# Choice over clusters kept in the PSUM bank of its logits, and new orders of steps for all engines

## The chip, the cores and the metric

The program runs on one core of one Trainium2 chip. The metric is the device time of one execution in microseconds, as the median of several runs. The core has five engines with a queue of instructions each: TensorE (PE in the profile), VectorE (DVE), ScalarE (ACT), GpSimd (POOL) and SyncE (SP), which here only issues loads and stores. ScalarE's queue issues some transfers too.

## What is computed

A layer on x of four batches of 512 tokens with 512 features (f32), in four stages, each of them `x = x + f(layernorm(x))`:

```python
attn = jnp.einsum('ds,td->st', w1, w2) * sparse_mask          # stage 1
y = jnp.einsum('bds,st->bdt', x, attn) + b2; gelu(y)
# stages 2 and 4 (the same weights)
dots = softmax(x @ centroids.T / 0.1, axis=-1)                # 64 clusters
hits = dots > 0.01
query_sel = any(hits, axis=1); cluster_sel = any(hits, axis=0)
dense = x @ weight.T + bias
out = where(query_sel[:, None] & cluster_sel[assignments][None, :], dense, 0)
# stage 3: attention with one head of 128: qkv, softmax(q k^T) v, Wo
```

`cluster_sel` is over all 2048 tokens of a stage, so the mask of the output columns is known only when the last batch's probabilities are.

## The kernel before

A tile is 128 tokens of one batch by 512 features; there are 16, named `b.t` (batch, tile). f32 products are made from three matmuls of operands split into a high and a low part (`products`, L1011 to L1020): high by high, low by high, high by low. A **chunk** is one block of 128 of the contraction, so three matmuls of 128x512.

What each engine does, and in which order, is written out in tables of steps: PE_ORDER, ACT_ORDER, DVE_ORDER, POOL_ORDER, SP_ORDER (loads and the stores issued by SyncE), AQ_ORDER (loads that ScalarE's queue issues first) and AS_ORDER (stores that it issues last). Each engine goes through its table strictly in order; a step waits on semaphores for what it needs (`done_at`). The names of the steps that matter here:

- `load.w1.c`, `load.w2.c`, `load.x0.t`: the loads of 256 KB with which the kernel starts. `w1hi.c`, `w2hi.c` (ScalarE, L590 and L586) copy the high part, `w1lo.c`, `w2lo.c` (VectorE) make the low one.
- `attn.c`: 12 matmuls of the product of the two weights (attn.0 in three parts of four); `last.i` ends that product for rows i.
- `stats`, `rstd`, `norm.s.b.t` (VectorE, GpSimd, ScalarE L613): layernorm of a tile; `T.xs.b.t` (TensorE, L1113): its transposition, four blocks into one of four rotating banks `t_bank`; `hi.x`, `lo.x` (ScalarE L645, VectorE L824) split it. `T.x2`, `T.x4` transpose what the stages 1 and 3 left, and their norm is applied after the product.
- `y1.b.t.cNN`, `dn2`, `dn4`: chunks NN of the products of the stages 1, 2 and 4 in one of four rotating banks `m_bank`; `dn4h.3.3.h` are the two halves of the last tile. The bank is freed by `x1`, `ev2`, `blend4`.
- The choice, for stage s (2 or 4) and batch b: `cls.b` (TensorE, L1197) makes the logits, 64 high and 64 low rows by 512 tokens; `lgev` (ScalarE, L681) copies them; `tc.s.b` (TensorE, L1119) transposes them into a `t_bank`; `logit` (VectorE, L930) adds high and low into `cl`; `lmax` (L935, L937) takes the maximum; `cexp` (ScalarE, L703) writes the exponentials into `ce`; `prob` (L944 to L954) sums, divides and takes the running maximum over batches. `best1` (L959), `bestT` (TensorE), `csel` and `mask.2`, or `tmask.4` and `masks.4` (L1138), then make the mask of the output columns.
- The end: `qb` and `xb` (ScalarE L755, GpSimd L559) put bias and residual together, `blend4` (L977) adds the product. For 11 tiles and the halves VectorE then copies by the mask (`out`, L1001; `outh`, L994); for the four tiles of BY_POOL GpSimd does it in two steps, `pm` (L565) with the mask in `rows` (ScalarE, `rows4`, L713), and `pa` (L570).

TensorE starts with WARM matmuls on constants (L1009), before any load has landed.

The body of prob before:

```python
link(dve.tensor_reduce(out=csum[:, :], in_=ce[:, :, :], op=ALU.add, axis=AX.X))
link(dve.reciprocal(crec[:, :], csum[:, :]))
dve.tensor_scalar(chosen, crec[:, :], THRESHOLD, None, ALU.is_gt).then_inc(chosen_done, 1)
```

(`link` makes VectorE wait for the instruction's own end.)

## Time and profile before

| | us |
|---|---|
| median of 3 runs (275.39 to 275.49) | 275.45 |
| the profiled execution | 275.24 |
| its span, first to last instruction | 273.4 |
| TensorE busy (1397 matmuls) | 268.8 |
| VectorE busy | 192.2 |
| ScalarE busy | 177.0 |
| GpSimd busy | 163.8 |

All times inside the span count from its start. Matmuls overlap each other in the trace, so that what one costs is read from the distance of the starts, not from its duration. Idle time of an engine matters only where TensorE, or the last store, waits for it.

### The profile page before, as it was taken

What the parts mean: (1) busy time and instruction counts of PE and PEld (TensorE: products, weight loads), DVE (VectorE), ACT (ScalarE), POOL (GpSimd) and SP (SyncE); (2) the same over time, 40 slices, a digit from 0 to 9 for tenths busy, and PEclk for the clock granted to TensorE, in tenths of its full rate; (3) what the DMA queues carried; (4) which work ended last, traced back from release to release, by engine and by line L of the source; (5) the groups of instructions that cost most, each with busy time, mean ns of one, the idle gap of its engine ahead of it and who ended that gap; (6) DMA issues with size and microseconds to landing.
All of it is one profiled execution on the core that took longest, in us unless ns stands there. A gap on an engine that the chain in (4) does not pass through costs nothing.

```text
span 273.4 us, 4428 instructions
## 1 busy us (share of the span) xinstructions
PE 268.8 (98%) x1397; PEld 225.6 (82%) x1397; DVE 192.2 (70%) x406; ACT 177.0 (65%) x359; POOL 163.8 (60%) x196
## 2 busy tenths in 40 slices
PE   8999999999999999999999999999999999999995
PEld 8787888888888888788988888888888888887784
DVE  3988988605935867794478796788447584875994
ACT  3855886455477786448889988779544747577500
POOL 4883988265395491189896993990541247102795
PEclk9999999999999999999999999999999999999999
DMA  7999064800000000000000000000000000000096
GB/s 253 372 362 326 14 219 167 305 4 2 0 0 0 2 0 2 0 2 0 2 0 0 1 4 0 0 2 0 2 2 0 0 2 0 1 2 0 36 361 220
DMA packets 10247, 18.25 MB, mean 67 GB/s; under 512 B 1200, under 2 KB 1968, under 8 KB 10224
## 3 DMA queue, kind: packets, MB, share of 16 engines
q1 hardware_dynamic: 8784, 15.47, 16.2%
q10 hardware_dynamic: 1440, 2.49, 2.5%
q8 instruction: 12, 0.20, 0.3%
q14 instruction: 11, 0.09, 0.1%
HBM read 13.76 MB, written 4.19 MB: 66 GB/s over the span
## 4 chain that ended last, share of the span: by engine, by line
PE 96%; DMA 1%; DVE 1%; POOL 1%; issue 0%; ACT 0%; DVEq 0%; POOLq 0%
PE m_bank L1018 76%; PE t_bank L1113 12%; PE m_bank L1197 6%; PE t_bank L1119 1%; DMA x_tok<-in_L_attn_a_x 1%; PE m_bank L1073 1%; ACT xn_odd L613 0%; PE t_bank L1138 0%; DVE st L817 0%; POOL rstd L471 0%; POOL ve L470 0%; DVE y_tok L988 0%; DVE x_tok L994 0%; PE m_bank L1144 0%; PE t_bank L1124 0%
## 5 line engine op out<-in xcount | busy, mean ns | idle before, releaser
L1018 PE MATMUL m_bank<-ffn_hi,even_hi 128*128 128x512 f32 x96 | 38.9, 406 | 0.0
L1018 PE MATMUL m_bank<-ffn_lo,even_hi 128*128 128x512 f32 x96 | 37.6, 392 | 0.0
L1018 PE MATMUL m_bank<-ffn_hi,even_lo 128*128 128x512 f32 x96 | 37.4, 390 | 0.0
L602 ACT ACTIVATE ones_and_squares<-x_tok,mv 128x512 bf16<-128x512 f32 x44 | 31.6, 717 | 4.1 <-DVE x_tok L921 3.7
L559 POOL TENSOR_TENSOR y_tok<-y_tok,x_tok 128x512 f32<-128x512 f32 x12 | 15.3, 1289 | 25.6 <-ACT y_tok L755 25.6
L539 POOL TENSOR_TENSOR y_tok<-y_tok,bias_f 128x512 f32<-128x512 f32 x16 | 20.6, 1295 | 16.2 <-ACT y_tok L696 16.2
L467 POOL TENSOR_SCALAR ve<-mv 128x1 f32<-128x1 f32 (+1 forms) x20 | 5.3, 264 | 37.9 <-ACT ones_and_squares L602 36.9
L824 DVE TENSOR_TENSOR even_lo<-t_bank,even_hi 128x512 fp32r<-128x512 f32 x24 | 16.2, 684 | 12.8 <-ACT even_hi L645 12.6
L471 POOL TENSOR_TENSOR rstd<-ve,half 128x1 f32<-128x1 f32 (+1 forms) x31 | 23.5, 758 | 2.6
L824 DVE TENSOR_TENSOR odd_lo<-t_bank,odd_hi 128x512 fp32r<-128x512 f32 x28 | 18.8, 686 | 6.4 <-ACT odd_hi L645 6.2
L1018 PE MATMUL m_bank<-odd_hi,wqkv_hi 128*128 128x512 f32 (+1 forms) x60 | 21.5, 358 | 0.0
L1018 PEld LDWEIGHTS m_bank<-ffn_lo,even_hi 128*128 128x128 f32 x96 | 18.0, 188 | 3.9
L1018 PE MATMUL m_bank<-odd_lo,wqkv_hi 128*128 128x512 f32 (+1 forms) x60 | 20.9, 349 | 0.0
L553 POOL TENSOR_TENSOR x_tok<-x_tok,bo 128x512 f32<-128x512 f32 x16 | 20.9, 1322 | 0.0
L1018 PE MATMUL m_bank<-odd_hi,wqkv_lo 128*128 128x512 f32 (+1 forms) x60 | 20.8, 347 | 0.0
L1018 PEld LDWEIGHTS m_bank<-ffn_hi,even_lo 128*128 128x128 f32 x96 | 18.1, 189 | 3.1
L1018 PEld LDWEIGHTS m_bank<-ffn_hi,even_hi 128*128 128x128 f32 x96 | 18.1, 188 | 3.0
L613 ACT ACTIVATE xn_odd<-x_tok,ve,rstd 128x512 f32<-128x512 f32 x20 | 16.1, 811 | 5.8 <-POOL ve L474 5.8
L1018 PE MATMUL m_bank<-attn_hi,odd_hi 128*128 128x512 f32 x48 | 19.5, 406 | 0.0
L1018 PE MATMUL m_bank<-attn_lo,odd_hi 128*128 128x512 f32 x48 | 18.8, 392 | 0.0
L1018 PE MATMUL m_bank<-attn_hi,odd_lo 128*128 128x512 f32 x48 | 18.7, 390 | 0.0
L645 ACT ACTIVATE even_hi<-t_bank 128x512 fp32r<-128x512 f32 x24 | 13.8, 595 | 6.8 <-PE t_bank L1113 6.8
(191 smaller groups left out, 784.8 us busy)
## 6 DMA issues: line engine op xcount, KB each, us to landing
x_tok<-in_L_attn_a_x SPq DMA_DIRECT2D x3, 1024.0 KB, 9.8
xn_odd<-in_L_attn_a_xt SPq DMA_DIRECT2D x2, 1024.0 KB, 7.3
out<-x_tok ACTq DMA_DIRECT2D x8, 256.0 KB, 2.2
out<-x_tok SPq DMA_DIRECT2D x7, 256.0 KB, 2.2
x_tok<-in_L_attn_a_x SPq DMA_DIRECT2D x4, 256.0 KB, 4.1
w_raw<-in_L_attn_a_w SPq DMA_DIRECT2D x4, 256.0 KB, 5.0
xt_other<-in_L_ffn_weight SPq DMA_DIRECT2D x4, 256.0 KB, 5.9
y_tok<-in_L_attn_a_sparse_mask SPq DMA_DIRECT2D x4, 256.0 KB, 6.5
```

What stands on the lines that cost most here:

```text
L467: link(pool.tensor_scalar(ve[:, i:i + k], mv[:, i:i + k, 1], 1.0 / D ** 3, EPS, ALU.mult, ALU.add))
L471: ins = pool.tensor_tensor(rstd[:, i:i + k], ve[:, i:i + k], half[:, 0:k], ALU.pow)
L539: pool.tensor_tensor(y_tok[:, n, :], y_tok[:, n, :], bias_f[:, :], ALU.add).then_inc(done[kind], 1)
L553: pool.tensor_tensor(x_tok[:, n, :], x_tok[:, n, :], bo[:, :], ALU.add).then_inc(done[kind], 1)
L559: pool.tensor_tensor(y_tok[:, n, :], y_tok[:, n, :], x_tok[:, n, :], ALU.add).then_inc(done[kind], 1)
L602: act.activation(squares, x_tok[:, n, :], ACT.Square, bias=sum_of(*key), scale=-float(D), accum_out=mv[:, i, 1:2]).then_inc(done[kind], 1)
L613: act.activation(xn_odd[:, t, :], x_tok[:, n, :], ACT.Identity, bias=nbias[:, i:i + 1], scale=rstd[:, i:i + 1]).then_inc(done[kind], 1)
L645: act.activation(split_of(what, b, t)[0], bank_view(what, bank_of("T", *key)), ACT.Copy).then_inc(done[kind], 1)
L824: dve.tensor_tensor(lo, bank_view(what, bank_of("T", *key)), f32(hi), ALU.subtract).then_inc(done[kind], 1)
L1018: ins = pe.matmul(bank, a, w, start=(first and n == 0), stop=(last and n == count - 1))
L1113: ins = pe.transpose(bank[:, c * r:(c + 1) * r], blk, ident[0:r, 0:r])
L1197: ins = pe.matmul(bank[:, tokens], cen_hl[:, c, :], a[:, c, tokens], start=(c + h == 0), stop=(c == KC - 1 and h == 1))
```

## The change

All tables of steps are new. Apart from them:

```diff
-WARM = 12
+WARM = 10
-AQ_ORDER = "load.w1.0"
+AQ_ORDER = """
+load.w1.0 load.x0.0
+"""
+        def choice_in(stage, b):
+            bank = bank_of("tc", stage, b)
+            small = [bank[:, TPB * (NC + i):TPB * (NC + i + 1)] for i in range(3)]
+            return bank[:, 0:TPB * NC].rearrange("p (t c) -> p t c", t=TPB), *small
...
-                        ins = act.activation(ce[:, k, :], cl[:, k, :], ACT.Exp, bias=ncmx[:, k:k + 1],
+                        ins = act.activation(choice_in(*key)[0][:, k, :], cl[:, k, :], ACT.Exp, bias=ncmx[:, k:k + 1],
...
-                    link(dve.tensor_reduce(out=csum[:, :], in_=ce[:, :, :], op=ALU.add, axis=AX.X))
-                    link(dve.reciprocal(crec[:, :], csum[:, :]))
-                    dve.tensor_scalar(chosen, crec[:, :], THRESHOLD, None, ALU.is_gt).then_inc(chosen_done, 1)
-                    link(dve.tensor_tensor(cl[:, :, :], ce[:, :, :], crec[:, :].unsqueeze(2).broadcast_to([P, TPB, NC]),
-                                           ALU.mult))
-                    dve.wait_ge(chosen_done, COUNT[kind][key])
+                    weights, _, total, share = choice_in(*key)
+                    link(dve.tensor_reduce(out=total, in_=weights, op=ALU.add, axis=AX.X))
+                    dve.reciprocal(crec[:, :], total).then_inc(shared, 1)
+                    link(dve.reciprocal(share, total))
+                    dve.tensor_scalar(chosen, share, THRESHOLD, None, ALU.is_gt)
                     if stage == 4:
-                        dve.tensor_tensor(rq[:, 1, b * TPB:(b + 1) * TPB], rstd[:, i:i + TPB], chosen, ALU.mult)
+                        dve.scalar_tensor_tensor(out=rq[:, 1, b * TPB:(b + 1) * TPB], in0=share, scalar=THRESHOLD,
+                                                 in1=rstd[:, i:i + TPB], op0=ALU.is_gt, op1=ALU.mult)
+                    dve.wait_ge(shared, COUNT[kind][key])
+                    link(dve.tensor_tensor(weights, weights, crec[:, :].unsqueeze(2).broadcast_to([P, TPB, NC]), ALU.mult))
...
-            freed_by = {"T": "lo", "tc": "logit", "bestT": "csel", "last": "mask_attn", "y1": "x1", "dn2": "ev2",
+            freed_by = {"T": "lo", "tc": "prob", "bestT": "csel", "last": "mask_attn", "y1": "x1", "dn2": "ev2",
```

The maximum of `lmax` goes into the same bank. `ce`, `cmx` and `csum` are gone.

Where the tables move work, at the places that the text below speaks of:

TensorE at the start, before (L1073 is attn.0, L1113 a transpose, L1018 attn.1 and what follows):

```order
L1009 MATMUL m_bank<-ones_and_squares 128x128 x12
L1073 MATMUL m_bank<-w2t_hi,even_hi 128x512 x4
L1113 MATMUL t_bank<-ident,xn_odd 128x128 x4
L1073 MATMUL m_bank<-w2t_lo,even_hi 128x512 x4
L1073 MATMUL m_bank<-w2t_hi,even_lo 128x512 x4
L1113 MATMUL t_bank<-ident,xn_odd 128x128 x4
L1018 MATMUL m_bank<-w2t_hi,even_hi 128x512
L1018 MATMUL m_bank<-w2t_hi,even_lo 128x512
L1018 MATMUL m_bank<-w2t_lo,even_hi 128x512
L1018 MATMUL m_bank<-w2t_hi,even_hi 128x512
L1018 MATMUL m_bank<-w2t_hi,even_lo 128x512
L1018 MATMUL m_bank<-w2t_lo,even_hi 128x512
```

and now (L1075 is attn.0, L1020 attn.1; the transposes follow only after its twelve matmuls):

```order
L1011 MATMUL m_bank<-ones_and_squares 128x128 x10
L1075 MATMUL m_bank<-w2t_hi,even_hi 128x512 x4
L1075 MATMUL m_bank<-w2t_hi,even_lo 128x512 x4
L1075 MATMUL m_bank<-w2t_lo,even_hi 128x512 x4
L1020 MATMUL m_bank<-w2t_hi,even_hi 128x512
L1020 MATMUL m_bank<-w2t_hi,even_lo 128x512
L1020 MATMUL m_bank<-w2t_lo,even_hi 128x512
L1020 MATMUL m_bank<-w2t_hi,even_hi 128x512
L1020 MATMUL m_bank<-w2t_hi,even_lo 128x512
```

Both transposes of the first tiles have moved behind attn.1, and the part with w2t_lo now comes last.

ScalarE at the start, before (L590 is w1hi, L586 w2hi, L613 the normalization of a tile):

```order
L576 DMA y_tok<-in_L_attn_a_w 128x512
L590 ACT_TABLE_LOAD
L590 ACTIVATE even_hi<-y_tok 128x512
L586 ACTIVATE w2t_hi<-w_raw 128x512
L613 ACTIVATE xn_odd<-x_tok,ve,rstd 128x512
L590 ACTIVATE even_hi<-y_tok 128x512
L613 ACTIVATE xn_odd<-x_tok,ve,rstd 128x512
L586 ACTIVATE w2t_hi<-w_raw 128x512 x2
L590 ACTIVATE even_hi<-y_tok 128x512 x2
L586 ACTIVATE w2t_hi<-w_raw 128x512
L613 ACTIVATE xn_odd<-x_tok,ve,rstd 128x512
```

and now:

```order
L581 DMA y_tok<-in_L_attn_a_w 128x512
L581 DMA x_tok<-in_L_attn_a_x 128x512
L590 ACT_TABLE_LOAD
L590 ACTIVATE even_hi<-y_tok 128x512
L586 ACTIVATE w2t_hi<-w_raw 128x512
L590 ACTIVATE even_hi<-y_tok 128x512
L586 ACTIVATE w2t_hi<-w_raw 128x512
L613 ACTIVATE xn_odd<-x_tok,ve,rstd 128x512
L586 ACTIVATE w2t_hi<-w_raw 128x512
L590 ACTIVATE even_hi<-y_tok 128x512 x2
L586 ACTIVATE w2t_hi<-w_raw 128x512
L613 ACTIVATE xn_odd<-x_tok,ve,rstd 128x512 x2
```

The first normalization stands behind four copies instead of two, the next two behind all eight, and ScalarE's queue issues a second load.

TensorE between the logits of batch 2 in stage 4 and their transposition, before (L1197 are the last logits matmuls, L1113 transposes of x4 tiles, L1119 is tc.4.2):

```order
L1197 MATMUL m_bank<-even_hi,cen_hl 128x512
L1197 MATMUL m_bank<-even_lo,cen_hl 128x512
L1113 MATMUL t_bank<-ident,x_tok 128x128 [waits x3_done,lo_done]
L1113 MATMUL t_bank<-ident,x_tok 128x128 x3
L1113 MATMUL t_bank<-ident,x_tok 128x128 [waits x3_done,lo_done]
L1113 MATMUL t_bank<-ident,x_tok 128x128 x3
L1119 MATMUL t_bank<-ident,lg 128x128 [waits lgev_done,lo_done]
L1119 MATMUL t_bank<-ident,lg 128x128 x3
```

and now (L1199, L1115, L1121):

```order
L1199 MATMUL m_bank<-even_hi,cen_hl 128x512
L1199 MATMUL m_bank<-even_lo,cen_hl 128x512
L1199 MATMUL m_bank<-even_hi,cen_hl 128x512
L1199 MATMUL m_bank<-even_lo,cen_hl 128x512
L1115 MATMUL t_bank<-ident,x_tok 128x128 [waits x3_done,lo_done]
L1115 MATMUL t_bank<-ident,x_tok 128x128 x3
L1121 MATMUL t_bank<-ident,lg 128x128 [waits lgev_done,lo_done]
L1121 MATMUL t_bank<-ident,lg 128x128 x3
```

One transposed tile instead of two stands between the logits and tc.4.2, and the next logits follow directly.

GpSimd at the end, before (L559 is xb, L565 pm, L570 pa):

```order
L467 TENSOR_SCALAR ve<-mv 128x4
L471 TENSOR_TENSOR rstd<-ve,half 128x4
L559 TENSOR_TENSOR y_tok<-y_tok,x_tok 128x512 x5
L565 TENSOR_TENSOR y_tok<-y_tok,rows 128x512
L570 TENSOR_TENSOR x_tok<-x_tok,y_tok 128x512
L565 TENSOR_TENSOR y_tok<-y_tok,rows 128x512
L570 TENSOR_TENSOR x_tok<-x_tok,y_tok 128x512
L565 TENSOR_TENSOR y_tok<-y_tok,rows 128x512
```

and now (L564, L570, L575):

```order
L558 TENSOR_TENSOR x_tok<-x_tok,bo 128x512
L564 TENSOR_TENSOR y_tok<-y_tok,x_tok 128x512
L472 TENSOR_SCALAR ve<-mv 128x4
L476 TENSOR_TENSOR rstd<-ve,half 128x4
L564 TENSOR_TENSOR y_tok<-y_tok,x_tok 128x512 x4
L570 TENSOR_TENSOR y_tok<-y_tok,rows 128x512 x2
L575 TENSOR_TENSOR x_tok<-x_tok,y_tok 128x512 x2
L570 TENSOR_TENSOR y_tok<-y_tok,rows 128x512
L564 TENSOR_TENSOR y_tok<-y_tok,x_tok 128x512
L575 TENSOR_TENSOR x_tok<-x_tok,y_tok 128x512
L570 TENSOR_TENSOR y_tok<-y_tok,rows 128x512
L575 TENSOR_TENSOR x_tok<-x_tok,y_tok 128x512
```

One xb (of tile 3.3) now stands between the steps pm and pa, and one more xb comes early, before the last batch's choice.

## Rows read from the trace of the kernel before

**Rows 1.** The page: busy time by engine; the granted clock in 40 slices.

```profile
PE 268.8 (98%) x1397; PEld 225.6 (82%) x1397; DVE 192.2 (70%) x406; ACT 177.0 (65%) x359; POOL 163.8 (60%) x196
...
PEclk9999999999999999999999999999999999999999
```

**Rows 2.** Timeline, TensorE, 0 to 14 us: start, us, engine, line, operation, idle before.

```profile
0.97 5.49 PE L1009 MATMUL m_bank<-ones_and_squares 128*128 128x128 f32 x24 [0.97 <-POOL ones_and_squares L446]
...
6.12 1.31 PE L1073 MATMUL m_bank<-w2t_hi,even_hi 128*128 128x512 f32 x4
...
6.59 0.62 PE L1073 MATMUL m_bank<-w2t_hi,even_hi 128*128 128x512 f32 x2
...
7.67 0.66 PE L1113 MATMUL t_bank<-ident,xn_odd 128*128 128x128 f32 x4 [0.25 <-ACT xn_odd L613]
...
13.24 0.60 PE L1113 MATMUL t_bank<-ident,xn_odd 128*128 128x128 f32 x4
```

**Rows 3.** Timeline of SyncE's issues, then DMA issues by stretch (last column: us to landing).

```profile
1.15 0.42 SPq L397 DMA_DIRECT2D w_raw<-in_L_attn_a_w  x1
...
3.51 0.98 SPq L397 DMA_DIRECT2D w_raw<-in_L_attn_a_w  x2
...
w_raw<-in_L_attn_a_w SPq DMA_DIRECT2D x1, 256.0 KB, 3.7
...
w_raw<-in_L_attn_a_w SPq DMA_DIRECT2D x2, 256.0 KB, 5.0
```

**Rows 4.** Timeline, ScalarE, 4 to 12 us.

```profile
4.90 0.63 ACT L586 ACTIVATE w2t_hi<-w_raw 128x512 fp32r<-128x512 f32 x1
...
8.15 0.82 ACT L613 ACTIVATE xn_odd<-x_tok,ve,rstd 128x512 f32<-128x512 f32 x1
...
9.91 1.18 ACT L590 ACTIVATE even_hi<-y_tok 128x512 fp32r<-128x512 f32 x2
```

**Rows 5.** Timeline, TensorE, around tc.4.2 (243.76) and tc.4.3 (248.74).

```profile
242.82 1.03 PE L1113 MATMUL t_bank<-ident,x_tok 128*128 128x128 f32 x8
243.76 0.63 PE L1119 MATMUL t_bank<-ident,lg 128*128 128x128 f32 x4
...
248.27 0.39 PE L1018 MATMUL m_bank<-ffn_lo,even_hi 128*128 128x512 f32 x1
248.74 0.63 PE L1119 MATMUL t_bank<-ident,lg 128*128 128x128 f32 x4
```

**Rows 6.** The chain that ended last, in order of time: start, us, what.

```profile
70.90 5.47 PE m_bank L1018 x24
...
242.99 0.87 PE t_bank L1113 x8
...
257.12 13.12 PE m_bank L1018 x69
```

**Rows 7.** Timeline of GpSimd, ScalarE and the two queues, 250 to 273.4 us.

```profile
254.86 5.05 POOL L559 TENSOR_TENSOR y_tok<-y_tok,x_tok 128x512 f32<-128x512 f32 x4 [2.83 <-ACT y_tok L755]
...
269.11 1.28 POOL L570 TENSOR_TENSOR x_tok<-x_tok,y_tok 128x512 f32<-128x512 f32 x1
...
257.16 0.60 ACT L713 ACTIVATE rows<-t_bank 128x512 f32<-128x512 f32 x1
...
270.43 0.42 ACTq L769 DMA_DIRECT2D out<-x_tok  x1
...
271.33 0.33 SPq L391 DMA_DIRECT2D out<-x_tok  x1
```

**Rows 8.** Timeline, VectorE, 252 to 255 us (prob.4.3 and best1.4).

```profile
252.78 0.18 DVE L945 RECIPROCAL crec<-csum 128x4 f32<-128x4 f32 x1
...
254.06 0.63 DVE L959 TENSOR_REDUCE best<-best 128x64 f32<-128x256 f32 x1
```

**Rows 9.** DMA issues of the last stretches: size, us to landing.

```profile
out<-x_tok ACTq DMA_DIRECT2D x1, 256.0 KB, 2.2
...
out<-x_tok SPq DMA_DIRECT2D x1, 128.0 KB, 1.7
```

205 lines of the change are left out of this document (99 added, 106 removed).

## The prediction

> **What bounds the kernel now.** First the page. TensorE is busy 268.8 us, 98% of a span of 273.4 us [rows 1], and the chain of work that ended last runs over TensorE from its first transpose to its last matmul (three of its pieces in [rows 6]). So the other engines matter only where TensorE stands still, at the start and at the end. Second, the timeline of TensorE at the start [rows 2]: the warm-up matmuls run from 0.97 us, the first real one starts at 6.12, the next at 6.59, and the chain shows the transpose of the first normalized tile at 7.67 after an idle stretch. At 13.24 us the parts attn.0 and attn.1 (24 matmuls) and two transposes are done. Third, the issue and landing of the loads [rows 3] and ScalarE's work at the start [rows 4]. Fourth, the timeline of TensorE around the logits of the last two batches [rows 5]: two matmuls of 128x512 that follow each other are 0.228 us apart (24 in 5.47 us, [rows 6]), but from the start of the last matmul before the transposes tc.4.3 to these there are 0.47 us. Last, the tail [rows 7]: the last matmuls, GpSimd's queue and the last stores.
>
> The profiled execution took 275.24 us, 1.84 more than its span, and the median of the runs is 275.45. I sum against 275.24 and add 0.21 at the end.
>
> **The start.** The warm-up loses 2 of 12 matmuls. The twelve last from 0.97 to 6.12 us, 0.43 each, so the ten end at 5.27: up to 0.86 us freed [rows 2]. Before, ScalarE had w2hi.0 done at 4.90 + 0.63 = 5.53 [rows 4], so the warm-up held the first product back by some 0.5 us. This is no longer so, but the new first loads set a bound of their own. x0.0 moves to ScalarE's queue behind w1.0 and now runs beside w2.0. w2.0 landed third, 3.7 us after its issue at 1.15, so at 4.85; the ninth load (w2.2) was issued at 4.0 (the second of the pair at 3.51) and landed 5.0 later, at 9.0; that is 0.69 us for each 256 KB between them [rows 3]. Shared with x0.0, w2.0 lands between 4.85 and 5.54, and the first product starts between 5.6 and 6.2. Both ends give the same sum, because a later wait takes up the difference: the transpose T.x1.0.0 now stands behind attn.1 and T.x1.0.2, and its normalization stands on ScalarE behind the four copies w2hi.3, w1hi.2, w1hi.3, w2hi.2. w2.3 is now the ninth load and lands at 9.0 to 9.1. Four copies at 0.58 (two in 1.18, [rows 4]) and a normalization of 0.82 end at 9.1 + 2.3 + 0.8 = 12.3; a transposed tile takes 0.44 (two in 0.87, [rows 6]), so the same 24 matmuls and two transposes are done at 12.77 instead of 13.24. **Gain 0.45**, bounds 0.2 and 0.7, by 0.25 either way in the landing of one load. Of what is moved on SyncE's queue, the first sparse mask stays the 17th load, so at about 14.1, when last.0 ends; rstd.1.0.3 stands behind three sums on GpSimd (each as long as one xb, 1.26, [rows 7]), but its transpose is wanted only at 20 us, 6 us after these can start.
>
> The Trainium skill, page "DMA: Bandwidth & Descriptors", section "Queues, rings and completion order", says that a DMA engine goes round-robin between its queue rows packet by packet. By that w2.0 lands at 5.5 and not at 4.85. The sum above is the same with either.
>
> **The middle.** The 1397 matmuls are the same but for the warm-up; what can change is where TensorE stands still. From the timeline I find these waits after 13.24 us: three of 0.24 in front of tc.2.3, tc.4.3 and the masks of stage 4 (0.47 instead of 0.228, one pattern, [rows 5]); 0.07 at tc.4.2 (0.94 from the first transpose of the pair to tc.4.2, where two take 0.87); and some 0.3 in pieces under 0.1. In all 1.1. The new order puts two chunks of a product (three matmuls each, 0.684) instead of one in front of tc.2.3, tc.4.3 and the masks, which is more than the 0.24 that lacked. These three waits go: 0.72. In front of tc.4.2 stands one transpose instead of two. The copy of the logits on ScalarE must end in between, and the 0.94 stay, with 0.44 of cover: a wait of 0.50 instead of 0.07. Of the small pieces I let 0.15 go. Net of what is counted: 0.72 - 0.43 + 0.15 = **0.45 gained**.
>
> The new order has some hundred other places where a bank or a split tile must be ready. I counted for each the TensorE work between producer and consumer. The tightest are as tight as the tightest of before (1.81 us from a transpose to its product, as before), except these: T.x2.3.3 has 2.05 us to cl2.3.h1, where before the closest had 3.2, and VectorE has two reductions of the choice to do first, which leaves about 0.2; dn4.0.0 has 1.12 us until its bank is wanted, and VectorE must blend it in between; T.x1.0.0 is in the sum already. Bounds 0 and 1.0 for all such waits, **0.1 taken**, since the order of before has the same kind of tightness and no wait at all from 116 to 242 us.
>
> **The choice over clusters.** Its exponentials, maximum, sum and products now lie in the bank of the transposed logits. The bank is freed by prob instead of logit, some 4.5 us later; the next user of each such bank comes 12.9 us of TensorE work after it or later, so nobody waits. On VectorE a second reciprocal comes in (0.18, [rows 8], and less from start to start where nothing is linked) and the small product for rq moves out of the gap between multiplication and maximum: 0.1 us more per batch, 8 times. Behind it are queued the splits and blends of VectorE, and best1 for bestT. Between tc.4.3 and bestT.4 there are nine chunks, 6.15 + 0.44 us, as before, against 5.95 from tc.4.3 at 248.74 to the end of best1 at 254.69 [rows 5, 8]; 0.1 more is covered. I have no row for such small operands in PSUM; taking a fifth more or less on each of six steps of 0.2 to 0.4 us, I bound that at -0.3 to +0.3 per batch, on the path only if over 0.5. **0**.
>
> **The end.** tmask.4 and masks.4 change places and stand nearer to the end: 13 chunks and the two halves follow them, where 15 did. The 15 and the halves took 13.12 us [rows 6], so now 13.12 - 2 x 0.684 + 0.23 = 12.0 from the start of the second mask matmul, 12.2 from the first, masks.4. Before, rows4 started on ScalarE at 257.16 and took 0.60, about 0.4 after its matmul's start, and GpSimd was the slower one anyway: four xb in 5.05 us until 259.9 and then eight steps without a gap, the last from 269.11 to 270.39, 1.32 each, while TensorE ended at 257.12 + 13.12 = 270.24 [rows 6, 7]. Now rows4 is done at 0.4 + 0.6 after masks.4, at E - 11.2 (E is the end of TensorE), and behind it GpSimd has the eight steps and xb.3.3: 8 x 1.32 + 1.26 = 11.8. It ends at E + 0.6 instead of E + 0.14. Its last store, issued at 270.43 before, took 2.2 us to landing; the last half from VectorE was issued at 271.33, which is E + 1.08, and took 1.7, so it landed at E + 2.8 [rows 7, 9]. The store behind GpSimd now lands at E + 0.6 + 2.2 = 2.8 too, and the two overlap: at 0.69 for 256 KB the 384 KB want 1.0 us of the DMA engines, which puts the later one at up to E + 3.2. **Loss 0.2**, bounds 0 and 0.5. VectorE's eleven masked copies start 1.2 us later relative to E; at a rough 0.65 each, they and four blends take 9.8 us from E - 11.5, so it waits for TensorE again before the last halves.
>
> **Sum.** 275.24 - 0.45 - 0.45 + 0.1 + 0.2 = 274.64 by the profiled execution, 274.8 to 274.85 as a median. I say **274.8**.
>
> **The rivals.** (a) *The gain is spent on new waits and the tail*: the 0.2 left at T.x2.3.3 is not there, two or three places like dn4.0.0 cost 0.2 each, and the last stores cost 0.4 to 0.5. Then the two gains of 0.45 meet 0.9 of losses: 275.0 to 275.6, no change. For it: the order of before has its waits in three of seven such chains, and the new one is drawn as tight. Against: the long dense stretch of before. Chance 0.33. (b) *The clock, slower than before*: in the warm-up each 128x128 f32 matmul takes 0.43 us, and the first real one is followed after 0.47, the later ones after 0.23 [rows 2]; the granted clock reads full speed, 2.4 GHz, in every slice [rows 1], so the trace does not settle why. If TensorE works at its low level until about 6.5 and the level depends on what it did before, then two warm-up matmuls fewer and a hole of 0.3 to 0.9 us before the first product can leave the next ones at the low level. Each costs 0.24 us; 0.45 + 0.25 of net gain are gone after three, and ten of them give 275.45 + 2.4 - 0.6 = 277.2. Against: 4.3 us of warm-up remain, of 5.15. Chance 0.12, around 276.5. The Trainium skill, page "TensorE: Matmul & The Clock Gate", section "What's actually happening", says that the throttled state is the default and activity releases it. By it the weaker warm-up is a risk and no saving, as in (b); by the rows of before alone it is a saving. (c) *More is gained*: no new waits, the tail as before, the small pieces gone too: 275.45 - 0.5 - 1.0 = 273.9. Chance 0.12. (d) *The choice in PSUM does nothing*: it is so in my forecast already.
>
> **How the numbers follow.** Forecast 0.43 (274.4 to 274.95), (a) 0.33, (c) 0.12, (b) 0.12. This kernel can be told from no change at about 0.2%, 0.55 us, so faster means under 274.9: (c), most of the forecast: 0.50. Same: the rest of the forecast and (a): 0.36. Slower: (b) and the upper end of (a): 0.14. The range takes in (c) and (a) and leaves out (b) and the fringe of (c): 273.9 to 275.8.
>
> **What would show it.** In the trace of after: T.x1.0.0 is the first TensorE wait behind attn.1, and last.0 starts near 12.8 (wrong if past 13.3); attention matmuls 0.47 apart past 6.6 us would be (b); tc.2.3, tc.4.3 and the masks follow without a gap, and tc.4.2 after a gap of 0.5; GpSimd's last step ends 0.4 to 0.7 after the last matmul. If a gap of over 0.3 stands anywhere from 30 to 240 us, my count of the places was too kind.

## The result and the profile after

| | before | after |
|---|---|---|
| median, us | 275.47 (275.39 to 275.65) | 277.21 (276.93 to 277.32) |
| ratio, 95% interval | | 1.0063 (1.0047 to 1.0079) |
| span of the profiled execution | 273.4 | 275.3 |
| start of the last matmul | 269.95 | 271.83 |
| TensorE busy | 268.8 | 269.2 |

The change makes the kernel 1.74 us slower, where I had forecast 0.65 faster. The last matmul comes 1.88 us later, so that the loss lies ahead of it and the tail costs nothing. The page shows as little of it as before: TensorE busy 98%, full granted clock everywhere.

```profile
PE 269.2 (98%) x1393; PEld 225.7 (82%) x1393; DVE 194.0 (70%) x414; ACT 180.8 (66%) x361; POOL 164.5 (60%) x196
...
PEclk9999999999999999999999999999999999999999
```

The loss is in TensorE's timeline. The start (columns as in [rows 2]):

```profile
0.98 4.63 PE L1011 MATMUL m_bank<-ones_and_squares 128*128 128x128 f32 x20 [0.98 <-POOL ones_and_squares L451]
6.25 2.04 PE L1075 MATMUL m_bank<-w2t_hi,even_hi 128*128 128x512 f32 x4 [0.64 <-issue]
8.10 1.91 PE L1075 MATMUL m_bank<-w2t_hi,even_lo 128*128 128x512 f32 x4
9.80 1.22 PE L1075 MATMUL m_bank<-w2t_lo,even_hi 128*128 128x512 f32 x4
...
13.61 1.04 PE L1115 MATMUL t_bank<-ident,xn_odd 128*128 128x128 f32 x8
14.41 0.47 PE L1020 MATMUL m_bank<-w2t_hi,even_hi 128*128 128x512 f32 x1
```

The first product starts at 6.25 behind an idle stretch of 0.64 us. Then four matmuls take 1.85 us and the next four 1.70, 0.46 and 0.43 each, and only from about 9.9 us on they stand 0.23 apart. Before, this step came at 6.6 [rows 2]. The 24 matmuls and two transposes are done at 14.41, where the kernel before had them at 13.24 and I expected 12.77: 1.17 us lost, with the sign that rival (b) named. The granted clock reads full in every slice of the page, so only the distances, which halve at the step, show two levels of TensorE; I read them as its two clocks.

The largest wait of the middle, at T.x3.1.0, in the timelines of TensorE, ScalarE and GpSimd:

```profile
140.19 0.63 PE L1115 MATMUL t_bank<-ident,xn_odd 128*128 128x128 f32 x4 [0.86 <-ACT xn_odd L613]
...
136.57 0.19 ACT L602 ACTIVATION_READ_ACCUMULATOR ones_and_squares<-x_tok,mv 128x1 f32 x1
138.75 0.60 ACT L645 ACTIVATE odd_hi<-t_bank 128x512 fp32r<-128x512 f32 x1 [2.00 <-PE m_bank L1020]
139.25 0.80 ACT L613 ACTIVATE xn_odd<-x_tok,ve,rstd 128x512 f32<-128x512 f32 x1
...
136.56 0.27 POOL L479 TENSOR_SCALAR ve<-mv,rstd 128x1 f32<-128x1 f32 x1
```

The transpose comes 1.03 us late and waits for its normalization (ScalarE, L613, 139.25). Its rstd was there at 136.83 (L479). But in ScalarE's order hi.x3.1.3 stands ahead of it, which waits until the last product of batch 0's v has read the split tiles. ScalarE stood idle for 2.00 us with the wanted step second in its queue. Before, norm.3.1.0 stood behind hi.x3.1.3 too, but TensorE wanted T.x3.1.0 last of the four, two transposes and two parts of a product after v.0; now only sc.0.2 stands between.

tc.4.2, and the end on TensorE, GpSimd and SyncE's queue:

```profile
245.50 0.60 PE L1115 MATMUL t_bank<-ident,x_tok 128*128 128x128 f32 x4
246.44 0.63 PE L1121 MATMUL t_bank<-ident,lg 128*128 128x128 f32 x4 [0.34 <-ACT lg L681]
...
271.83 0.28 PE L1020 MATMUL m_bank<-ffn_lo,odd_hi 128*128 128x256 f32 x1
...
271.01 1.28 POOL L575 TENSOR_TENSOR x_tok<-x_tok,y_tok 128x512 f32<-128x512 f32 x1
...
273.20 0.33 SPq L396 DMA_DIRECT2D out<-x_tok  x1
```

tc.4.2 follows its one transpose after 0.94 where 0.44 would do: a wait of 0.50, as predicted. tc.2.3, tc.4.3 and masks.4 follow without a gap, as predicted; mask.2 has a new one of 0.22. GpSimd ends at 272.29, 0.2 behind TensorE, and the span ends 3.5 behind the start of the last matmul, as before. Sum of what is named: 1.17 + 1.03 + 0.43 + 0.22 - 0.72 = 2.13, less 0.25 in small pieces of both signs, makes the 1.88. Against the terms of the prediction: the start lost 1.17 instead of gaining 0.45, what was counted in the middle gained about 0.5 (forecast 0.45), the places that I had put at 0.1 in all lost 1.25 (1.03 and 0.22), and the end lost nothing (forecast 0.2).

### The profile page after: what moved, and what is told of

Same layout as the page of the kernel before. It is cut to its first block, busy times and chain, and to the rows that moved or that the text cites. A ratio compares the mean times of both kernels' runs of the same rounds, so it can differ in the third digit from the quotient of the medians.

```text
span 275.3 us, 4434 instructions
## 1 busy us (share of the span) xinstructions
PE 269.2 (98%) x1393; PEld 225.7 (82%) x1393; DVE 194.0 (70%) x414; ACT 180.8 (66%) x361; POOL 164.5 (60%) x196
## 4 chain that ended last, share of the span: by engine, by line
PE 97%; issue 1%; ACT 1%; DVE 0%; POOL 0%; ACTq 0%; DVEq 0%; POOLq 0%
PE m_bank L1020 75%; PE t_bank L1115 12%; PE m_bank L1199 5%; PE m_bank L1075 2%; PE m_bank L1011 2%; PE t_bank L1121 1%; ACT xn_odd L613 0%; ACT lg L681 0%; DVE y_tok L990 0%; PE m_bank L1146 0%; PE t_bank L1140 0%; DVE x_tok L996 0%; PE t_bank L1135 0%; PE t_bank L1136 0%; PE t_bank L1130 0%
## 5 line engine op out<-in xcount | busy, mean ns | idle before, releaser
L1020 PE MATMUL m_bank<-ffn_hi,even_hi 128*128 128x512 f32 x96 | 39.5, 411 | 0.0
L1020 PE MATMUL m_bank<-ffn_lo,even_hi 128*128 128x512 f32 x96 | 37.6, 392 | 0.0
L1020 PE MATMUL m_bank<-ffn_hi,even_lo 128*128 128x512 f32 x96 | 37.5, 390 | 0.0
L564 POOL TENSOR_TENSOR y_tok<-y_tok,x_tok 128x512 f32<-128x512 f32 x12 | 15.4, 1295 | 33.8 <-ACT y_tok L755 33.8
L824 DVE TENSOR_TENSOR even_lo<-t_bank,even_hi 128x512 fp32r<-128x512 f32 x24 | 16.2, 684 | 11.7 <-ACT even_hi L645 11.6
L645 ACT ACTIVATE even_hi<-t_bank 128x512 fp32r<-128x512 f32 x24 | 13.9, 594 | 11.8 <-PE t_bank L1115 7.8
L1020 PE MATMUL m_bank<-odd_hi,wqkv_hi 128*128 128x512 f32 (+1 forms) x60 | 21.6, 360 | 0.0
L1020 PEld LDWEIGHTS m_bank<-ffn_lo,even_hi 128*128 128x128 f32 x96 | 18.0, 188 | 3.9
L1020 PE MATMUL m_bank<-odd_lo,wqkv_hi 128*128 128x512 f32 (+1 forms) x60 | 20.9, 348 | 0.0
L1020 PE MATMUL m_bank<-odd_hi,wqkv_lo 128*128 128x512 f32 (+1 forms) x60 | 20.8, 347 | 0.0
L1020 PEld LDWEIGHTS m_bank<-ffn_hi,even_hi 128*128 128x128 f32 x96 | 18.1, 188 | 2.9
L1020 PEld LDWEIGHTS m_bank<-ffn_hi,even_lo 128*128 128x128 f32 x96 | 18.1, 189 | 2.8
L645 ACT ACTIVATE odd_hi<-t_bank 128x512 fp32r<-128x512 f32 x28 | 16.3, 601 | 5.5 <-PE t_bank L1115 3.5
L1020 PE MATMUL m_bank<-attn_hi,odd_hi 128*128 128x512 f32 x48 | 19.3, 402 | 0.0
L1020 PE MATMUL m_bank<-attn_lo,odd_hi 128*128 128x512 f32 x48 | 18.8, 392 | 0.0
L1020 PE MATMUL m_bank<-attn_hi,odd_lo 128*128 128x512 f32 x48 | 18.7, 389 | 0.0
## 6 DMA issues: line engine op xcount, KB each, us to landing
x_tok<-in_L_attn_a_x SPq DMA_DIRECT2D x3, 1024.0 KB, 10.3
out<-x_tok ACTq DMA_DIRECT2D x8, 256.0 KB, 2.3
out<-x_tok SPq DMA_DIRECT2D x7, 256.0 KB, 2.5
w_raw<-in_L_attn_a_w SPq DMA_DIRECT2D x4, 256.0 KB, 5.4
xt_other<-in_L_ffn_weight SPq DMA_DIRECT2D x4, 256.0 KB, 7.0
y_tok<-in_L_attn_a_sparse_mask SPq DMA_DIRECT2D x4, 256.0 KB, 7.6
```

The costliest lines, as they stand in the source:

```text
L564: pool.tensor_tensor(y_tok[:, n, :], y_tok[:, n, :], x_tok[:, n, :], ALU.add).then_inc(done[kind], 1)
L645: act.activation(split_of(what, b, t)[0], bank_view(what, bank_of("T", *key)), ACT.Copy).then_inc(done[kind], 1)
L824: dve.tensor_tensor(lo, bank_view(what, bank_of("T", *key)), f32(hi), ALU.subtract).then_inc(done[kind], 1)
L1020: ins = pe.matmul(bank, a, w, start=(first and n == 0), stop=(last and n == count - 1))
```

## The experiments

Each kernel was timed beside the kernel before on the same chip, whose medians there were 275.40 to 275.49 us (275.93 beside the two with wide warm-ups of experiment 6); `four_warm40` ran once and has no ratio. Medians are in us, ratios have their 95% interval. The kernels ran in groups on different chips, so medians of two groups are compared with more care than within one. "Span" is that of the timed executions.

**1. One wait mended, and the changed kernel once more.**

```diff
-norm.3.1.2 qkhi.k.0 qkhi.q.0 sq.3.2.1 hi.x3.1.3 norm.3.1.0 hi.x3.1.2 norm.3.1.1
+norm.3.1.2 qkhi.k.0 qkhi.q.0 sq.3.2.1 norm.3.1.0 norm.3.1.1 hi.x3.1.3 hi.x3.1.2
```

> The changed kernel with one edit in ScalarE's order: norm.3.1.0 and norm.3.1.1 stand ahead of hi.x3.1.3, which waits for the last product of v.0. Theory (the wait of 0.86 us at T.x3.1.0 comes from ScalarE's strict order, since the rstd of this tile was there 1.9 us before hi.x3.1.3 could start): the idle stretch near 139 to 140 us goes, nothing else moves, and the time falls by 0.7 to 1.0 us: 276.2 to 276.5 us. Rival (the time is given back at the next late step, the split of the transposed tiles for k.1 and q.1, or at the end): the gap goes, but another of 0.3 us or more comes up behind it and less than 0.5 us is gained.

Measured 276.37, ratio 1.0029 (1.0014 to 1.0043), 0.85 less than the changed kernel. The gap at 139 is gone, but another of 0.55 came up behind it: T.v.0.0 waits for the bank of T.x3.1.3, whose low part VectorE makes third of the four; it starts the first of them at 139.43, after a pause of 2.44 us. Both theories had a part: a second wait lay hidden behind the first. The two waits differ by 0.48 us only; the rest of the 0.85 comes from the start, which was early in this trace.

```profile
142.16 0.66 PE L1115 MATMUL t_bank<-ident,vt 128*128 128x128 f32 x4 [0.36 <-DVE odd_lo L824]
...
139.43 0.69 DVE L824 TENSOR_TENSOR odd_lo<-t_bank,odd_hi 128x512 fp32r<-128x512 f32 x1 [2.44 <-ACT odd_hi L645]
```

But the trace also showed the first matmuls 0.23 apart from 6.4 us on, with the same code at the start. So the changed kernel ran again:

> The changed kernel once more, unedited, as the measure for the three beside it and for one question: in the trace of its first execution TensorE's matmuls stood 0.43 to 0.47 us apart until 9.9 us, but in that of the changed kernel with only ScalarE's order edited at 139 us, whose start is the same code, they stood 0.23 us apart from the first. Theory now (the step to the full clock comes at a time that differs from execution to execution, and ten warm-up matmuls leave it to chance whether it comes before or behind the hole): this trace can show either, and the time is 276.9 to 277.3 us. Rival (the first trace is the rule): 0.43 to 0.47 us again until 9 us or later.

Measured 277.35, ratio 1.0063 (1.0050 to 1.0076). The theory held. The starts, and the two waits that then come up:

```profile
0.98 4.27 PE L1011 MATMUL m_bank<-ones_and_squares 128*128 128x128 f32 x20 [0.98 <-POOL ones_and_squares L451]
6.29 1.17 PE L1075 MATMUL m_bank<-w2t_hi,even_hi 128*128 128x512 f32 x4 [1.04 <-ACT w2t_hi L586]
...
12.72 0.66 PE L1115 MATMUL t_bank<-ident,xn_odd 128*128 128x128 f32 x4 [0.27 <-ACT xn_odd L613]
13.13 0.48 PE L1020 MATMUL m_bank<-w2t_hi,even_hi 128*128 128x512 f32 x1
...
20.95 0.66 PE L1115 MATMUL t_bank<-ident,xn_odd 128*128 128x128 f32 x4 [0.27 <-ACT xn_odd L613]
...
56.69 0.50 PE L1020 MATMUL m_bank<-ffn_hi,even_hi 128*128 128x512 f32 x1 [0.48 <-ACT y_tok L696]
...
51.89 1.67 ACT L661 ACTIVATE odd_hi<-xt_other 128x512 fp32r<-128x512 f32 x3 [2.23 <-DMA xt_other<-in_L_attn_a_xt]
...
52.60 1.30 POOL L514 TENSOR_TENSOR odd_lo<-xt_other,odd_hi 128x512 fp32r<-128x512 f32 x1 [7.47 <-ACT odd_hi L661]
53.98 0.20 POOL L472 TENSOR_SCALAR ve<-mv 128x4 f32<-128x4 f32 x1
```

The ten warm-up matmuls end at 5.25 instead of 5.61: the step of the clock fell into the warm-up, and a hole of 1.04 us behind it did no harm. The start is 1.28 us earlier (13.13 against 14.41), and yet the last matmul comes at 271.80, as in the first trace. The gift is taken back at two places: 0.43 us at T.x1.0.3 (its rstd stands on GpSimd behind three sums, the first of which waits for a load until 14.1) and 0.75 us at 56.7 (rstd.2.0 stands on GpSimd behind xlo.2.3, whose input lands at 51.9; before, it stood ahead of it).

The second of them is partly chance. The load in question (1 MB of xt), here and in `after_warm12` of experiment 2, which has the same orders and no wait at 57:

```profile
xt_other<-in_L_attn_a_xt SPq DMA_DIRECT2D x1, 1024.0 KB, 6.7
```

```profile
xt_other<-in_L_attn_a_xt SPq DMA_DIRECT2D x1, 1024.0 KB, 5.4
```

It lands after 5.2 to 5.5 us in 15 of the 20 traces and after 6.2 to 6.7 us in five (`after_again`, `after_norm`, `after_five`, `five_wide7`, `before_warm10`). On the changed orders TensorE then loses 0.2 to 0.75 us near 57 us; in `before_warm10`, with rstd.2.0 ahead, it loses nothing. Why the load is slower at times is open. So the low clock is not free: it hides the 0.43, and costs the changed kernel some 0.7 us of its 1.17 (experiment 2), unless a slow load takes these too.

**2. The warm-up.** `WARM = 12` in the changed kernel, with and without the edit of experiment 1; `WARM = 10` in the kernel before.

> The changed kernel with 12 warm-up matmuls instead of 10. In the changed kernel the first real matmul starts at 6.25 us after 0.64 us of idleness, and the first eight or so matmuls stand 0.43 to 0.47 us apart until 9.9 us. Theory (the clock: fewer warm-up matmuls and a hole behind them keep TensorE at its low level): the warm-up now reaches about 6.5 us, there is no hole, the matmuls stand 0.23 us apart from about 6.9 us on, and attn.0, attn.1 and two transposes are done at 13.1 to 13.5 us instead of 14.41 (the normalization of tile 0.0 is ready only at about 13.0, so it can't be less); 0.9 to 1.3 us less than the changed kernel: 275.9 to 276.3 us where that takes 277.2. Rival (the order of the first products and their loads makes them slow, not the clock): the distances stay 0.43 to 0.47 us until 9.9 us, and the time is that of the changed kernel or 0.2 us more.

> Both edits: 12 warm-up matmuls, and norm.3.1.0 and norm.3.1.1 ahead of hi.x3.1.3. Theory (the two losses at 6 to 14 us and at 139 us are all that made the changed kernel slower than predicted, and they add): 277.2 less 1.1 less 0.9 gives 275.2 us, bounds 274.8 and 275.5; that is no slower than the kernel before. Rival (a third loss stands in the middle or the end, the choice in PSUM among them): over 275.7 us.

> The kernel before with 10 warm-up matmuls instead of 12. Theory (the clock): the warm-up ends near 5.3 us, the first product can start near 5.6 us, and TensorE stays at its low level past 6.6 us: matmuls 0.43 to 0.47 us apart until 8 to 10 us, attn.0, attn.1 and two transposes done 0.3 to 1.2 us after the 13.24 of the kernel before, 275.8 to 276.6 us. Rival (the two warm-up matmuls fewer are a saving, as I predicted, and the slow start of the changed kernel has to do with its order): matmuls 0.23 us apart from 6.6 us at the latest, done at 12.8 to 13.2 us, 275.0 to 275.4 us.

Measured 277.22 (1.0067, 1.0055 to 1.0080), 276.66 (1.0047, 1.0034 to 1.0059) and 275.40 (1.0000, 0.9991 to 1.0009). With 12 the matmuls stand 0.23 apart from 6.4 us on, the two transposes are done at 13.31, and the last matmul of the first of them starts at 271.11, 0.72 earlier: so much of the 1.88 is the clock, and 1.16 is left with the full clock. The time did not fall, because the last stores landed after 2.5 us instead of 1.7 (experiment 5). The expected 275.2 for both edits missed by 1.5: 0.8 at the end, 0.4 at T.x1.0.3 and 0.5 at T.v.0.0, less small pieces. In the kernel before, two warm-up matmuls fewer change nothing, as the rival there had it: the first products stand 0.23 us apart from 6.7 us on, a wait for a normalization follows them in any case (0.44 instead of 0.25 us), and its 11 executions have spans of 273.5 to 273.8. There the warm-up ends at the low level too, but the first product follows it after 0.1 us.

**3. The waits of the orders, mended one by one.** `after_four` adds to experiment 1:

```diff
-lo.x3.1.2 max.0.2 lo.x3.1.0 lo.x3.1.3 lo.x3.1.1          (VectorE)
+lo.x3.1.3 lo.x3.1.2 max.0.2 lo.x3.1.0 lo.x3.1.1
-fsum.1 fsum.2 fsum.3 rstd.1.0.3                          (GpSimd)
+fsum.1 rstd.1.0.3 fsum.2 fsum.3
-T.x4.3.3 wo.3.2 cl4.2.h01 T.x4.3.2 tc.4.2                (TensorE)
+wo.3.2 cl4.2.h01 T.x4.3.3 T.x4.3.2 tc.4.2
```

with hi.x4.3.3 and lo.x4.3.3 moved behind lgev.4.2 and lo.x4.3.0. `after_three` leaves the last place out; `after_five` adds norm.1.0.0 ahead of w2hi.2 on ScalarE.

> The changed kernel with four places of the orders mended, 10 warm-up matmuls: norm.3.1.0 and norm.3.1.1 ahead of hi.x3.1.3; lo.x3.1.3 first among its four (the bank that T.v.0.0 waits for); rstd.1.0.3 behind one sum of GpSimd instead of three; and at tc.4.2 a second transposed tile, T.x4.3.3, between the logits and their transposition. Theory (each wait is local, the earlier ones hid the later ones, and together they are the loss): against the trace with only the norms mended, whose last matmul starts at 270.69, the waits of 0.41 at T.x1.0.3, 0.55 at T.v.0.0 and 0.50 at tc.4.2 go, less about 0.2 that comes up elsewhere: last matmul near 269.4, 276.4 - 1.2 = 275.1 us, bounds 274.7 and 275.5. Rival (what one wait gives back the next takes, as it was with the norms alone): 275.8 us or more.

> The kernel with three of the four places mended: the order at tc.4.2 is left as in the changed kernel (one transposed tile between the logits and their transposition). Theory (this wait was sized rightly in my prediction, 0.50 against 0.07, and it is on the path): the wait stands in the trace, and the time is 0.35 to 0.5 us more than with four, 275.2 to 275.4 us. Rival (the tail takes it up, since GpSimd ends within 0.2 us of TensorE): within 0.2 us of the kernel with four.

> The kernel with the four mended places and a fifth: on ScalarE norm.1.0.0 stands ahead of the copy w2hi.2, which waits for the last load of w2 (it lands at 11.5 us and was not in my sum), instead of behind it. Theory (this landing, not the ninth load, sets the transpose T.x1.0.0 and with it the start): the transpose comes at 12.3 to 12.5 us instead of 12.8 to 13.1, the first part of last.0 then needs the low part of w2.2 and starts 0.1 to 0.4 us earlier than the 13.2 to 13.5 of the traces with the full clock: 0.1 to 0.4 us less than the kernel with four, 274.5 to 274.8 us. Rival (the wait only moves to last.0, or to the next tile's transpose): the same time as with four, within 0.15 us.

Measured: four 274.89, ratio 0.9976 (0.9962 to 0.9990); three 275.96, 1.0031 (1.0013 to 1.0050); five 275.73, 1.0016 (0.9998 to 1.0034). The expectations of three (275.2 to 275.4) and five (274.5 to 274.8) were missed, that of four (274.7 to 275.5) was met. With four, the waits at the first three places are gone and that at tc.4.2 is down to 0.07, and the last matmul starts at 269.59: 2.2 us ahead of the changed kernel's, 0.36 ahead of the kernel before's. **It is the fastest kernel of the study**, 0.24% faster than before and 0.9% faster than the changed one. Since the start differs with the clock, the orders are best compared from the moment at which the 24 matmuls and two transposes are done:

| trace | done at | last matmul | between |
|---|---|---|---|
| before | 13.24 | 269.95 | 256.7 |
| after (low clock at the start) | 14.41 | 271.83 | 257.4 |
| after_warm12 | 13.31 | 271.11 | 257.8 |
| after_again (slow load) | 13.13 | 271.80 | 258.7 |
| after_four | 13.53 | 269.59 | 256.1 |
| after_four_warm11 | 13.28 | 269.30 | 256.0 |

At the full clock the changed orders take 1.1 us more than those of before, where I had forecast less, and with four places mended 0.6 us less. This is the main proof that waits of the orders, and with them not the clock alone, made the loss.

tc.4.2 alone gave less than its 0.50. Counted from the second tile's transposes (12.94 and 13.12), the last matmul comes after 256.57 us with three and after 256.47 with four. The trace of four shows where the rest went: wo.3.2, which now follows T.x4.3.1 at once, waits 0.21 us at 240.2, tc.4.2 itself 0.07, and the logits of the last batch 0.17. Most of what lies between the medians of three and four is elsewhere: the spans of three fall into two groups, six times 272.9 to 273.0 and four times 274.5 to 275.1, those of four from 272.6 to 274.1. Five has seven of twelve from 272.4 to 272.7, the shortest of all, and three from 274.0 to 274.9. The profiled execution of five was one of its long ones, with matmuls 0.46 us apart until 10 us; those of three and four were short ones, without it. The slow load has its part in it as well: TensorE lost 0.5 us at 57.7 in that trace. So the clock fits the two groups, but of most long executions there is no trace. With five and three there are also often 2.0 to 3.6 us around the span instead of 1.8. In the three traces with 2.8 to 2.9 us around it (`after_three`, `after_five`, `four_choice_undone`) TensorE's queue fetches one more packet of instructions 1.7 to 1.9 us behind the span's end (at 274.8, 276.7 and 276.8 us); none of the other 17, with 1.8 to 2.1 us, has one there. What decides it is open; these three ran on one chip and `after_four` on another, so the medians of four against three and five hold this difference too.

**4. The choice over clusters back outside PSUM** (`prob`, `lmax`, `cexp` and `freed_by` as in the kernel before), on the changed orders and on those of `after_four`.

> The changed kernel with the choice over clusters as before (its own buffers outside PSUM, the bank freed by logit, one reciprocal), all orders of steps and the warm-up as changed. Theory (the choice in PSUM does nothing for the time, as I predicted): within 0.3 us of the changed kernel, 276.9 to 277.4 us, and the distance between tc.4.3 and the masks unchanged. Rival (small operands in PSUM slow VectorE, or the later freeing of the bank holds something back): 0.4 us or more faster, under 276.8 us. Other rival (it is a gain hidden in the sum): over 277.5 us.

> The kernel with the four mended places, with the choice over clusters as before, outside PSUM. In the changed kernel with the choice undone, small steps of VectorE that touch no PSUM lasted 0.86, 1.10 and 1.40 us where they mostly last 0.16 to 0.42, one of them in front of the split that cl2.3 waits for (wait 0.54 us); with the choice in PSUM the same steps never last over 0.43. Theory now (in SBUF alone VectorE's steps are at times held up while GpSimd works, in PSUM they are not, and the new orders leave no room for that): 0.4 to 1.0 us more than the kernel with four, 275.3 to 275.9 us, and single steps of the choice of 0.6 us or more. Rival (my prediction, the choice in PSUM does nothing, and the slower run came from the clock at the start): within 0.25 us of the kernel with four, 274.7 to 275.1 us.

Measured 278.10 (1.0100, 1.0073 to 1.0127) and 277.33 (1.0066, 1.0040 to 1.0093): slower than their partners in PSUM by 0.75 (`after_again`) and 2.4 (`after_four`). The first is what the other rival there named; the second lies far above the expected 275.3 to 275.9. The choice of batch 2 in stage 2 with `four_choice_undone`, on VectorE, GpSimd and TensorE:

```profile
104.11 0.86 DVE L939 SCALAR_TENSOR_TENSOR ncmx<-cmx,rstd 128x4 f32<-128x4 f32 x1
...
103.93 1.98 POOL L534 TENSOR_TENSOR wqkv_lo<-y_tok,wqkv_hi 128x384 fp32r<-128x384 f32 x2
...
105.72 0.36 PE L1199 MATMUL m_bank<-odd_hi,cen_hl 128*128 128x256 f32 x1 [0.39 <-DVE odd_lo L826]
```

The step of 4 columns lasts 0.86 us instead of 0.16, until about the end of the first of GpSimd's two steps, and cl2.3.h1 comes 0.54 late. It is the place at which I had counted 0.2 us left. In the views by line (duration ns min/median/max), before, after, and with the choice undone:

```profile
L937 DVE SCALAR_TENSOR_TENSOR ncmx<-cmx,rstd x8: 161/163/666, 76.9 to 250.7; 128x4 f32<-128x4 f32 x8
L946 DVE TENSOR_SCALAR qsel<-crec x8: 169/170/632, 86.2 to 253.0; 128x4 f32<-128x4 f32 x8
```

```profile
L938 DVE SCALAR_TENSOR_TENSOR ncmx<-t_bank,rstd x8: 161/161/164, 69.4 to 253.5; 128x4 f32<-128x4 f32 x8
L949 DVE TENSOR_SCALAR qsel<-t_bank x8: 160/161/163, 78.4 to 255.9; 128x4 f32<-128x4 f32 x8
```

```profile
L948 DVE TENSOR_SCALAR qsel<-crec x8: 169/170/1104, 78.5 to 255.7; 128x4 f32<-128x4 f32 x8
L956 DVE TENSOR_TENSOR best<-best,cl x8: 416/422/1397, 79.0 to 256.3; 128x256 f32<-128x256 f32 x8
```

The last view is that of `four_choice_undone`. With the operands in SBUF a step of the choice is now and then held up, to 1.4 us; in the 15 traces with the choice in PSUM it never is. In the five traces with it in SBUF 16 such steps last over 0.6 us, and 13 of them end 0.02 to 0.03 us behind the end of a GpSimd instruction. That points to GpSimd as what holds them; no run takes it away. The Trainium skill, page "GPSIMD Engine Reference", section "8. Key points", says that GpSimd shares its SBUF interfaces with VectorE and contends with instructions in a 2-port mode or with two SBUF inputs. The traces agree for ncmx (0.86 us) and best (1.40 us), which have two SBUF inputs; whether qsel (1.10 us), with one, is in a 2-port mode no run here shows. To take the start out of the comparison:

> The kernel with four mended places and the choice over clusters as before, outside PSUM, with 24 warm-up matmuls of 32 columns, so that the clock at the start doesn't blur the comparison. Theory (VectorE's small steps of the choice are held up in SBUF, and it costs up to 0.9 us on the path): single steps of 0.6 to 1.4 us in the trace, spans spread over 273.3 to 274.5 us, median 275.3 to 276.0 us, 0.8 to 1.4 us more than the kernel with five places and the same warm-up. Rival (the slow executions of the last comparison were the clock alone): spans of 272.8 to 273.1 us, median 274.6 to 274.9 us.

Measured 282.00 (281.62 to 282.86; ratio 1.0239, 1.0221 to 1.0256), 0.57 more than `five_small24` with the same warm-up, and the wait of 0.54 at cl2.3.h1 again; the expected 275.3 to 276.0 was missed by the late start (experiment 6). The two differ in the fifth place also, but in both traces the 24 matmuls and two transposes are done at 19.66, so this doesn't blur the comparison. From there to the last matmul it is 0.60 us more with the choice outside PSUM, 0.70 between `four_choice_undone` and `after_four`, and 0.76 between `after_choice_undone` and the changed kernel. So on the new orders the choice in PSUM is worth 0.6 to 0.8 us, most of it the one wait. The edit also undoes the later freeing of the bank and the second reciprocal; these were not tried apart. Of the 2.4 of the other pair 1.2 is the start in its trace (14.71 against 13.53, products 0.46 us apart until 10 us), and some executions have the longer time around the span.

**5. The end.** The page counts TensorE's packets of instructions in a row of its own:

```profile
q8 instruction: 11, 0.18, 0.3%
```

```profile
q8 instruction: 12, 0.20, 0.3%
```

The row q8 is TensorE's: it alone changed when nothing but the number of warm-up matmuls did. Inside the span there are eleven packets with 10 warm-up matmuls of 128 columns and twelve with 11 or more, in the kernel before too. The Trainium skill, page "Runtime: NRT & Kernel Launch", section "Instruction fetch mechanics", gives blocks of 16 KiB that the engine's sequencer fetches by DMA while it goes on; 0.20 MB in twelve packets agree.

> The same with 11 warm-up matmuls. The kernels with 12 warm-up matmuls move a twelfth packet of 16 KB of instructions over a DMA engine 2 us before the last matmul, and their last stores land after 2.4 to 2.6 us instead of 1.7; those with 10 move eleven packets. Theory (the packet costs the 0.7 us at the end, and whether it is there depends on the number of TensorE's instructions): with 11 either there is no twelfth packet and the last stores land after 1.7 us, and the time is that of the kernel with 10 or 0.1 us less since the clock has risen by the first product; or there is one, and the time is 0.6 to 0.8 us more than with 10. Rival (12 warm-up matmuls cost at the end by another way): landing and number of packets don't go together.

> The kernel with five mended places and 12 warm-up matmuls of 128 columns. Theory: no hole, so no execution with the long span, but the twelfth packet of instructions goes beside the last stores, which land after 2.4 us instead of 1.7: spans of 273.0 to 273.6 us, all in one group, median 274.9 to 275.3 us. Rival (what is given back at the end hasn't to do with the packet): spans of 272.4 to 272.9 us.

> The kernel with the four mended places and 40 warm-up matmuls instead of 10: only the end matters here, the start is some 6 us late. Theory (the last stores land 0.7 us later where TensorE's twelfth packet of instructions goes over a DMA engine about 2 us before the last matmul): the twelfth packet now goes 5 us or more before the last matmul, the last stores land after 1.7 us again, and the span ends 3.5 us after the start of the last matmul. Rival (more than ten warm-up matmuls, or twelve packets, cost at the end whenever they go): landing 2.3 us or more, the span ends 4.2 us after the start of the last matmul.

| | twelfth packet | last matmul | last store lands after | span's end after last matmul |
|---|---|---|---|---|
| before | 267.5 | 269.95 | 1.7 | 3.5 |
| after_four | none | 269.59 | 1.7 | 3.5 |
| after_four_warm11 | 267.4 | 269.30 | 2.3 | 4.1 |
| after_warm12 | 269.4 | 271.11 | 2.5 | 4.2 |
| after_warm12_norm | 268.7 | 270.29 | 2.6 | 4.3 |
| five_warm12 | 267.5 | 269.21 | 2.5 | 4.2 |
| four_warm40 | 262.3 | 273.69 | 1.7 | 3.5 |
| five_small24 | 268.5 | 275.75 | 2.2 | 4.0 |

Measured 275.68 (1.0004, 0.9989 to 1.0019), 275.20 (0.9990, 0.9977 to 1.0004) and, once, 278.96; in all three the theory of the end held. (`five_warm12` was also to have no long execution, and one of its twelve has a span of 275.2.) The kernel of 24 narrow warm-ups (experiment 6) was to be harmless here and wasn't. On the changed orders the end is 0.6 to 0.8 us longer where the packet goes about 2 us ahead of the last matmul, 0.5 us longer at 7 us, and not longer at 11 us. In the kernel before it costs nothing 2.5 us ahead, though three stores ahead of the last one land later there than with ten warm-up matmuls (2.46 against 2.00 us for the first of them). The DMA rows from 268 to 280 us (0.3 us a digit) of the kernel before and of `after_warm12`, whose last matmuls start at 269.95 and 271.11, differ:

```profile
DMA  0079407955779692000000000000000000000000
```

```profile
DMA  9999999997895758969200000000000000000000
```

Before, the engines have pauses in which the one with the packet can catch up; on the new orders the masks come later and the stores are packed to the end. That is how I read it; no run separates the two.

**6. Other warm-ups.** 24 matmuls of 32 columns (below), then 7 of 512, to close the hole.

```diff
-pe.matmul(m_bank[M_BANKS - 1][:, 0:P], mean_raw[:, :], mean_raw[:, :], start=True, stop=True)
+pe.matmul(m_bank[M_BANKS - 1][:, 0:32], mean_raw[:, :], mean_raw[:, 0:32], start=True, stop=True)
```

> The kernel with five mended places, and 24 warm-up matmuls of 32 columns instead of 10 of 128. The kernels with 10 warm-up matmuls have two kinds of executions, spans of 272.4 to 273.0 us and of 274.3 to 275.1 us, and the two traces of the longer kind show the matmuls 0.46 us apart until 10 us. Theory (the hole behind the warm-up leaves it to chance whether the clock steps up at once or at 10 us, which costs 1.9 us; and 28 instructions more put TensorE's twelfth packet of instructions 3 us or more before the last matmul, where it delays no store): the warm-up has no hole of over 0.2 us behind it, no execution has the long span, the last stores land after 1.7 us: all spans within 272.4 to 272.9 us, median 274.3 to 274.6 us. Rival (the long kind has another cause, such as a load that lands late): spans of over 274 us in 2 or more of the executions.

> The changed kernel with 24 warm-up matmuls of 32 columns instead of 10 of 128, its orders untouched. Theory (with the clock up from the first product and no packet beside the last stores only the waits of the orders are left): the last matmul starts at 271.1 us as with 12 warm-up matmuls, not at 271.8, the span ends 3.5 us later at 274.6, median 276.4 us, bounds 276.2 and 276.8; so 0.8 us of the 1.8 by which the changed kernel is slower is the warm-up and 1.0 the orders. Rival (the later waits at 21 and 57 us take up what the clock gives): 277.0 us or more.

> The kernel with four mended places, and 7 warm-up matmuls of 512 columns instead of 10 of 128. [...] Theory (the slow executions are those in which the clock had not risen by the end of the warm-up): the wide warm-up raises it by 5 us at the latest in every execution; it ends at 5 to 7 us, none of the spans is over 273.6 us, the median 274.6 to 274.9 us and the highest under 275.6. Rival (the rise comes at a time of its own, whatever the warm-up is made of): again 2 to 4 of 12 spans of 273.8 us or more.

> The same warm-up with the fifth place mended too. Of the kernel with five places most spans were 0.3 to 0.4 us shorter than with four (272.4 to 272.7 against 272.6 to 273.1), but the time around the span was 2.5 to 3.0 us instead of 1.8, for a reason that I don't know. Theory: no long spans, all within 272.3 to 272.9 us; with 1.8 us around them 274.2 to 274.6 us, and with 2.8 around them 275.2. Rival: 2 or more of the executions have spans over 273.8 us.

All four missed: 281.43 (ratio 1.0209), 282.46 (1.0252), 277.38 (1.0053) and 277.37 (1.0059). A warm-up matmul of 32 columns takes as long as one of 128 at the low level, 0.43 us in two passes, so that 24 end at 11.2; and TensorE is still at the low level behind them. The stretches with 24 narrow ones, and with 40 of 128 columns (the first bracket has the passes that touch the stretch, one or two more than start in it, and in the fast stretch some three more):

```profile
4.00:5.00 1.00, 1.00 (x6) 1.00 (x7) 0.42 (x1) 0.32 (x1) 0.00 (x0) 1.00 1.07 414
9.00:10.00 1.00, 1.00 (x7) 1.00 (x6) 0.64 (x2) 0.57 (x3) 0.82 (x3) 1.00 1.10 313
```

```profile
2.00:3.00 1.00, 1.00 (x6) 1.00 (x6) 0.00 (x0) 0.93 (x1) 0.75 (x5) 1.00 0.56 106
4.00:5.00 1.00, 1.00 (x12) 1.00 (x11) 0.40 (x1) 0.29 (x1) 0.00 (x0) 1.00 1.05 406
```

With the narrow ones the passes start 0.21 us apart throughout, and then the products stand 0.43 to 0.46 apart for 3.6 to 4.4 us more in the three traces; with 40 of 128 columns they start 0.21 apart and from about 3.8 us on 0.11 apart. In that trace the granted clock reads 1.00 before and after the step: the column doesn't show it. The wide ones take 0.85 us a pass at first and 0.43 after the step, which comes near 4.4 us in one trace and near 7 in the other, and end at 8.4 and 9.7; I had priced them at half of that. Their spans lie in one group each, 275.3 to 275.9 and 275.0 to 276.4, but the late start hides what was to be seen. So no warm-up that closes the hole at no cost was found. `after_small24` against `five_small24` still says something: the medians differ by 1.03 us, and from the two transposes (19.29 and 19.66) to the last matmul it is 257.3 against 256.1 us. So the orders alone differ by 1.2 us where the late start hides the waits at 21 and 57 us.

## Why the prediction was wrong

The forecast added -0.45 for the start, -0.45 for the middle, +0.1 for all other places and +0.2 for the end. Two of these terms failed, the start and the 0.1; the other two were near.

- **"0.1 taken" for the other places, bounds 0 and 1.0**, is the step that failed by its mechanism: measured 1.03 at T.x3.1.0 alone (with 0.55 hidden behind it) and 0.22 at mask.2, and with an early start 0.43 at T.x1.0.3 and at times up to 0.75 at 56.7. I had counted TensorE's work between a producer and its consumer, but not what stands ahead of the producer in its own engine's order. At T.x3.1.0 and at 56.7 the wanted step was ready to run and stood behind one that waited; at T.x1.0.3 its input was there at 14.31, and three sums stood ahead until 18.2. The trace of before, in which nothing waits there, does not bound what a new order does.
- **The warm-up** ("the warm-up loses 2 of 12 matmuls", and rival (b) at 0.12) is the second: counted as a saving, it left the first eight products at the low level in the profiled execution, as (b) had it. But (b) is not the cause of the loss as a whole: the low level costs 0.7 us of the 1.88, and 1.16 are left at the full clock. That (b)'s sum of 277.2 is the measured time is luck, since it has none of the waits of the orders. The step comes at a time that differs from execution to execution, from 3.8 us to 7 in these traces, and near 10 in four (the changed kernel, five, and the two of experiment 4), where the ten warm-up matmuls ended at the low level with a hole behind them. The Trainium skill, page "TensorE: Matmul & The Clock Gate", section "What you observe", says that the moment of the transition varies from run to run, by half a microsecond either way; here it varies by far more, and the measurement decides. I had weighed only that it comes.
- **"Gain 0.45" at the start**: at the full clock it was 0.11 at best (13.13 against 13.24) and none with 12 warm-up matmuls (13.31). Beside the clock, the term that was wrong is "four copies and a normalization end at 12.3": I timed them from w2.3's landing at 9.1 (measured 9.3), but the fourth copy needs w2.2, the twelfth load, which landed at 11.7, so the normalizations began at 12.26. (By its own numbers the sum gives 12.2.) w2.0 landed at 5.5, at the late end of what I had allowed. `after_five` moves the fourth copy behind a normalization and has the shortest spans.
- **"Its transpose is wanted only at 20 us, 6 us after these can start"**: 4.1 us of sums, 1.8 of rstd and 0.8 of normalization need 6.7 from 14.1 on, where the load for the first sum is there. 0.43 us.
- **The middle, "0.45 gained"**: right in each piece (three waits gone, tc.4.2 0.50), but the latter, mended alone, gave some 0.1.
- **The choice, "0"**: 0.6 to 0.8 us gained on the new orders; on those of before it was not tried. The bound "-0.3 to +0.3 per batch, on the path only if over 0.5" missed single steps of 0.63 and 0.67 us that the trace of before held (above) and whose median hides them.
- **The end, "loss 0.2"**: 0.0 with eleven packets. GpSimd ended 0.2 behind TensorE and not 0.6, because its nine steps took 11.4 us and not 11.8, and the last stores landed after 2.1 and 1.7 us without holding each other up. The twelfth packet, which costs 0.5 to 0.8 us where it is there, was in no term.

## What to carry to other kernels

Where every engine goes strictly through its own order, look for each step on the critical path at what stands ahead of it on its engine, how long that lasts and what it waits for. The first wait found hides the next ones, so mend until the trace has none left, and look at more than one trace, since loads and the clock differ from execution to execution. Read the maximum of a small step besides its median; where it is far above, try an operand outside the memory that GpSimd is working in. A few instructions more or less can move a packet of instructions beside the last stores; compare the end, too, before an edit at the start is judged.

## What was new of the hardware

- TensorE's step from the low to the high level (passes 0.21 and then 0.11 us apart, products 0.46 and then 0.23) came before 5 us or near 10 behind the same ten warm-up matmuls, while the granted clock reads 1.00 all along. Behind 48 passes of 32 columns in 10.3 us it had not come in any of three traces.
- At the low level a warm-up pass (plain f32) takes 0.21 us with 32 columns as with 128, and 0.85 with 512.
- One packet of 16 KB of instructions about 2 us ahead of the last matmul goes with an end that is 0.6 to 0.8 us longer on the new orders, and with none in the kernel before. In three traces such a packet came 1.7 to 1.9 us behind the span's end, and these have 1 us more around the span than others.
- Steps of VectorE's choice over clusters of 0.16 to 0.42 us last up to 1.40 us with all operands in SBUF, and never over 0.43 with one in PSUM; 13 of the 16 held ones end 0.02 to 0.03 us behind a GpSimd instruction.
- The same load of 1 MB landed after 5.2 to 5.5 us in 15 traces and after 6.2 to 6.7 us in five.
